# Transposed probabilities of a causal attention: eight tiles a group become six, with V's first 64 tokens copied for the packed half

## The chip, the cores and the metric

The kernel runs on one core of one Trainium2 chip. The metric is the device time of one execution in microseconds (us), as the median of the runs shown.

## The reference, cut to what matters

The program is one transformer layer over 64 sequences ("batches") of 128 tokens and 1024 channels. A token stage builds the input h; then attention and a feed-forward part are added to it:

```
h = tok(log_dt, Lambda, x)                       # 64 x 128 x 1024
h = h + attn(layernorm(h), Wq, Wk, Wv, Wo)
h = h + ffn(layernorm(h), A, B, Wr, br)

# attn: 32 query heads in 8 groups of 4; a group shares one key head and one value head; head size 32
scores = einsum('bhqd,bhkd->bhqk', q, k_h) / sqrt(32)
scores = where(causal, finfo.min, scores)        # query t sees keys 0..t only
attn   = softmax(scores)
ctx    = einsum('bhqk,bhkd->bhqd', attn, v_h)
return ctx @ Wo
```

## The kernel before, in words

A first stage (some 245 us) makes h and the weights. The layer stage then works on one batch of 128 tokens at a time. Values are held as a high and a low f16 part, and products are the sum of three: high by high, high by low and low by high.

The causal mask leaves the first 64 queries with the first 64 keys only. So in each group the scores are computed in four tiles of 128 rows, where a row is one of two heads and one of 64 queries: two *lower* tiles (queries 0 to 63, 64 keys) and two *upper* tiles (queries 64 to 127, 128 keys). One group g of batch b goes through this chain:

1. TensorE: `scores`, four matmuls (L930) of 64, 64, 128 and 128 columns.
2. VectorE: `mask_min`, mask and row minimum, four instructions (L1206).
3. ScalarE: `exps`, four exponentials with their sums (L1062).
4. VectorE: `reciprocals` (L1214).
5. GpSimd: `normalise`, the probabilities by the reciprocals (L1427), over all 512 columns of `pr`. The two stretches of 64 columns that the lower tiles don't fill were set to zero once, before the loop.
6. ScalarE: `p_high`, the f16 part (L1072).
7. GpSimd: `p_low`, the rest in f16 (L1435).
8. The sync queue (SP): `p_transpose`, one DMA transpose of eight 128x128 tiles, four high and four low, into `pt[g]` (L868).

When all eight groups are transposed, `values` (L945) multiplies V by them. The output of a group is 32 rows high, so four groups lie side by side in the array's columns, and a *round* is four matmuls, one for each group. A half of the heads takes three rounds of 512 columns, so a batch takes six rounds, 24 matmuls. `ctx_high` (ScalarE, L1080) and `ctx_low` (VectorE, L1220) take the result, and the output projection (L902 to L904) uses it.

All of it is software-pipelined by hand. Each engine has a `body(i)` that lists the steps of several batches in a fixed order, and semaphores tie the engines. In TensorE's body `values(i - 1)` stands between pieces of the query projection of batch i + 1 (L916). In VectorE's body `reciprocals(i, 4)` is followed by `residual2(i - 3, 0)` (L1338), which empties the bank `pd` after the first three matmuls of the feed-forward output (L1008 to L1010); the second three need that bank.

Of the kernel before, what the change touches and what calls it, by code (L numbers as in the profile page):

```python
# [14 lines left out]
f16 = mybir.dt.float16  # L15
# [4 lines left out]
P = 128  # L20
# [626 lines left out]
def layer_stage(nc, h0, out, W, h_sent, ln_in):  # L647
# [5 lines left out]
    with ExitStack() as ctx:  # L653
# [6 lines left out]
        def ps(name):  # L660
# [25 lines left out]
        vf = sb("vf", [P, G * HD])  # L686
        v_hi = [sb(f"v_hi{i}", [P, G * HD], f16) for i in range(2)]
        v_lo = [sb(f"v_lo{i}", [P, G * HD], f16) for i in range(2)]
        smin = [sb(f"smin{i}", [P, HG]) for i in range(2)]
        pr = [sb(f"pr{i}", [P, HG * P]) for i in range(2)]  # L690
        rsum = [sb(f"rsum{i}", [P, HG]) for i in range(2)]
        rinv = [sb(f"rinv{i}", [P, HG]) for i in range(2)]
        p16 = [sb(f"p16{i}", [P, 2 * HG * P], f16) for i in range(2)]
        pt = [sb(f"pt{i}", [P, 2 * HG, P], f16) for i in range(RP)]
        ctx_t = [sb(f"ctx_t{i}", [P, 2 * G, P], f16) for i in range(2)]
# [61 lines left out]
        kl_done = sem("kl_done")  # L757
        vl_done = sem("vl_done")
        p_norm = sem("p_norm")

        TILES = tuple((h, pair, slice((2 * h + pair) * P, (2 * h + pair) * P + (HT, P)[h]))
                      for h in range(2) for pair in range(HG // 2))

# [30 lines left out]
        with nc.Block() as block:  # L794
# [102 lines left out]
            def _(pe):  # L897
# [36 lines left out]
                def values(b, odd):  # L934
                    if not has(b):
                        return
                    reached(pe, vl_done, 1, b, 1)
                    reached(pe, ctxl_done, G // 4, b)
                    for g in range(G):
                        landed(pe, b, g)  # L940
                    for m in range(G // 4):
                        for n, (v, lo) in enumerate(((v_hi[odd], 0), (v_lo[odd], 0), (v_hi[odd], HG))):
                            for g in range(4 * m, 4 * m + 4):
                                strip = slice(HD * (g % 4), HD * (g % 4) + HD)
                                last = pe.matmul(pv_ps[m][strip, :], v[:, g * HD:(g + 1) * HD],  # L945
                                                 pt[g][:, lo:lo + HG, :], start=(n == 0), stop=(n == 2))
                        last.then_inc(pv_done, 1)
# [105 lines left out]
            def _(act):  # L1053
# [84 lines left out]
                def v_high(b, odd):  # L1138
                    if not has(b):
                        return  # L1140
                    reached(act, kv_used, 1, b, 1)
                    reached(act, pv_done, G // 4, b - 1)
                    A.activation(v_hi[odd][:, :], vf[:, :], ACT.Copy).then_inc(vh_done, 1)

# [51 lines left out]
            def _(dve):  # L1196
# [13 lines left out]
                def reciprocals(b, g):  # L1210
                    if not has(b):
                        return
                    reached(dve, exp_done, G, b, g + 1)
                    V.reciprocal(rinv[g % 2][:, :], rsum[g % 2][:, :]).then_inc(rinv_done, 1)  # L1214
# [153 lines left out]
                def body(i, odd):  # L1368
# [46 lines left out]

                for i in range(2):
                    V.memset(pr[i][:, :].rearrange("p (t k) -> p t k", t=HG)[:, 0:2, HT:P], 0.0)
                bodies(dve, body)

            @block.gpsimd  # L1420
            def _(pool):
                def normalise(b, g):
                    if not has(b):
                        return
                    reached(pool, rinv_done, G, b, g + 1)
                    p3 = pr[g % 2][:, :].rearrange("p (j k) -> p j k", j=HG)
                    nc.gpsimd.tensor_tensor(p3, p3, rinv[g % 2][:, :].unsqueeze(2).broadcast_to([P, HG, P]),  # L1427
                                            ALU.mult).then_inc(p_norm, 1)

                def p_low(b, g):  # L1430
                    if not has(b):
                        return
                    reached(pool, ph_done, G, b, g + 1)
                    p = p16[g % 2]
# [36 lines left out]
                def v_low(b, odd):  # L1471
                    if not has(b):
                        return
                    reached(pool, vh_done, 1, b, 1)
                    nc.gpsimd.tensor_tensor(v_lo[odd][:, :], vf[:, :], v_hi[odd][:, :], ALU.subtract).then_inc(vl_done, 1)

# [61 lines left out]
```

## Time and profile before

| | |
|---|---|
| median of 3 runs | 2345.7 us (2343.22 to 2347.69) |
| the profiled execution's own time | 2347.87 us |
| its span | 2345.8 us |
| batches in the layer stage | 64 |
| granted TensorE clock, mean | 0.984 |

The span is divided by the profile into busy time of the engines. TensorE is busy for 95% of it, VectorE, ScalarE and GpSimd for 74 to 78%. A busy share says how full an engine is, not who waits for whom; for that the waits and the order of time are read. In the rows, PE is TensorE's matmuls, PEld its weight loads, DVE is VectorE, ACT is ScalarE and POOL is GpSimd. A matmul's duration in a row contains the time for which its result is still on the way, so a stream is read by the distance from start to start.

### The profile page before, as it was taken

What the parts mean: (1) busy time and instruction counts of PE and PEld (TensorE: products, weight loads), DVE (VectorE), ACT (ScalarE), POOL (GpSimd) and SP (SyncE); (2) the same over time, 40 slices, a digit from 0 to 9 for tenths busy, and PEclk for the clock granted to TensorE, in tenths of its full rate; (3) what the DMA queues carried; (4) which work ended last, traced back from release to release, by engine and by line L of the source; (5) the groups of instructions that cost most, each with busy time, mean ns of one, the idle gap of its engine ahead of it and who ended that gap; (6) DMA issues with size and microseconds to landing.
All of it is one profiled execution on the core that took longest, in us unless ns stands there. A gap on an engine that the chain in (4) does not pass through costs nothing.

```text
span 2345.8 us, 49764 instructions
## 1 busy us (share of the span) xinstructions
PE 2223.9 (95%) x14040; PEld 1160.3 (49%) x14040; DVE 1831.2 (78%) x7750; ACT 1752.2 (75%) x6141; POOL 1729.0 (74%) x1550
## 2 busy tenths in 40 slices
PE   3998699999999999999999999999999999999985
PEld 2886244544444444544454444444444444444442
DVE  8999467878877787777787778777777778777763
ACT  5887478777777777777877777777777777777772
POOL 3775488777777777777877777777777777777771
PEclk9999799999999999999999999999999999999987
DMA  3988699999999999999999999999999999999993
GB/s 95 291 270 257 118 173 190 188 192 191 186 196 196 187 190 194 193 184 193 197 187 193 194 184 193 193 189 190 191 186 193 200 188 191 194 186 187 184 174 81
DMA packets 1205662, 443.12 MB, mean 189 GB/s; under 512 B 1155718, under 2 KB 1158022, under 8 KB 1205388
## 3 DMA queue, kind: packets, MB, share of 16 engines
q1 hardware_dynamic: 1205380, 439.93, 95.7%
q8 instruction: 114, 1.87, 0.3%
q14 instruction: 160, 1.31, 0.2%
q10 hardware_dynamic: 8, 0.01, 0.0%
HBM read 87.43 MB, written 67.11 MB: 66 GB/s over the span
## 4 chain that ended last, share of the span: by engine, by line
PE 30%; POOL 17%; DMA 15%; DVE 11%; SPq 7%; issue 5%; ACT 4%; POOLq 0%; ACTq 0%; DVEq 0%
DMA pt<-p 11%; POOL p L1435 8%; POOL pr L1427 5%; PE pb L916 5%; PE pa L916 5%; PE pc L916 4%; SPq L868 3%; DMA h_ln<-h 3%; DVE xs L1267 3%; DVE pr L1206 2%; ACT p L1072 2%; POOL qr L1446 2%; PE pb L902 2%; PE pa L902 2%; PE pa L903 2%
## 5 line engine op out<-in xcount | busy, mean ns | idle before, releaser
L1062 ACT ACTIVATE pr<-pr,smin 128x64 f32<-128x64 f32 (+1 forms) x2048 | 737.8, 362 | 181.7 <-DVE smin L1206 180.6
L1427 POOL TENSOR_TENSOR pr<-pr,rinv 128x512 f32<-128x512 f32 x512 | 556.7, 1094 | 369.4 <-DVE rinv L1214 368.8
L1435 POOL TENSOR_TENSOR p<-pr,p 128x512 f16<-128x512 f32 x512 | 590.6, 1158 | 82.4 <-ACT p L1072 81.5
L1206 DVE CUSTOM_DVE_ANT_0 pr<-s_ps,cst 128x64 f32<-128x64 f32 (+1 forms) x2048 | 404.1, 252 | 239.4 <-POOL p L1435 146.2
L1072 ACT ACTIVATE p<-pr 128x512 f16<-128x512 f32 x512 | 320.0, 625 | 267.7 <-DMA pt<-p 146.7
L1062 ACT ACTIVATION_READ_ACCUMULATOR pr<-pr,smin 128x1 f32 x2048 | 383.5, 187 | 0.0
L916 PE MATMUL pa<-wkv_hi,xt 128*128 128x512 f16 x1024 | 326.7, 380 | 17.7 <-DMA xt<-xs 17.7
L916 PE MATMUL pb<-wq_hi,xt 128*128 128x512 f16 x1024 | 327.4, 381 | 0.0
L916 PE MATMUL pc<-wq_hi,xt 128*128 128x512 f16 x1024 | 315.0, 379 | 0.0
L640 PE MATMUL hps<-z,xw 128*128 128x256 f32 x792 | 177.9, 385 | 54.6 <-POOL xw L366 38.2
L902 PE MATMUL pb<-wo_hi,ctx_t 128*128 128x512 f16 x512 | 194.2, 379 | 4.2 <-DVE ctx_t L1220 3.7
L916 PE MATMUL pb<-wq_lo,xt 128*128 128x512 f16 x512 | 195.7, 382 | 0.0
L916 PE MATMUL pa<-wkv_lo,xt 128*128 128x512 f16 x512 | 195.6, 382 | 0.0
L902 PE MATMUL pa<-wo_hi,ctx_t 128*128 128x512 f16 x512 | 194.9, 381 | 0.0
L903 PE MATMUL pa<-wo_lo,ctx_t 128*128 128x512 f16 x512 | 194.8, 380 | 0.0
L904 PE MATMUL pa<-wo_hi,ctx_t 128*128 128x512 f16 x512 | 194.8, 380 | 0.0
L904 PE MATMUL pb<-wo_hi,ctx_t 128*128 128x512 f16 x512 | 194.3, 379 | 0.0
L903 PE MATMUL pb<-wo_lo,ctx_t 128*128 128x512 f16 x512 | 194.3, 379 | 0.0
L916 PE MATMUL pc<-wq_lo,xt 128*128 128x512 f16 x512 | 194.0, 379 | 0.0
L640 PEld LDWEIGHTS hps<-z,xw 128*128 128x128 f32 x792 | 150.9, 192 | 81.2 <-POOL xw L366 44.2
L930 PEld LDWEIGHTS s_ps<-kt,qt 128*128 128x128 f16 x2048 | 121.9, 98 | 130.2 <-DVE smin L1206 30.2
L930 PE MATMUL s_ps<-kt,qt 128*128 128x64 f16 (+1 forms) x2048 | 171.9, 207 | 11.0 <-DVE smin L1206 5.4
(178 smaller groups left out, 4730.2 us busy)
## 6 DMA issues: line engine op xcount, KB each, us to landing
h<-rows SPq DMA_DIRECT2D x128, 256.0 KB, 4.0
h_res<-h SPq DMA_DIRECT2D x64, 512.0 KB, 4.5
out<-rows SPq DMA_DIRECT2D x64, 512.0 KB, 3.3
h_ln<-h SPq DMA_DIRECT2D x63, 512.0 KB, 4.5
pt<-p SPq DMA_TRANSPOSE x512, 4.0
xa<-x SPq DMA_DIRECT2D x16, 256.0 KB, 4.2
xb<-x SPq DMA_DIRECT2D x32, 128.0 KB, 3.9
wst<-wq SPq DMA_DIRECT2D x8, 512.0 KB, 4.8
```

The lines of the kernel that those rows point to most:

```text
L640: last = pe.matmul(hps[t % 4][:, QROW * i:QROW * i + QROW], xw[w % XWR][:, t % WIN, 2 * i:2 * i + 2, :], z[g % ZR][:, 2 * (t % 2) + m, :], ...
L868: sp.dma_start_transpose(pt[g % RP][:, :, :], p16[g % 2][:, :]).then_inc(pt_in[g % RP], 16)
L902: pe.matmul(bank, x[:, k, :], w_hi[:, k, cols], start=(k == 0), stop=False)
L903: pe.matmul(bank, x[:, k, :], w_lo[:, k, cols], start=False, stop=False)
L904: last = pe.matmul(bank, x[:, KC + k, :], w_hi[:, k, cols], start=False, stop=(k == KC - 1))
L916: last = pe.matmul(bank, x[:, k if n < 2 * KC else KC + k, :], w[:, k, cols], start=(n == 0), stop=(n == 3 * KC - 1))
L930: last = pe.matmul(s_ps[g % 2][:, cols], qt[h][:, head:head + 2, :], kt[:, g, 0:HT * h + HT], start=True, stop=True)
L1062: last = A.activation(p, p, ACT.Exp, bias=smin[g % 2][:, j:j + 1], scale=-1.0, accum_out=rsum[g % 2][:, j:j + 1])
L1072: A.activation(p16[g % 2][:, 0:HG * P], pr[g % 2][:, :], ACT.Copy).then_inc(ph_done, 1)
L1206: V.tensor_tensor_reduce(pr[g % 2][:, cols], s_ps[g % 2][:, cols], masks[h], 1.0, 3e38, ALU.add, ALU.min, smin[g % 2][:, j:j + 1]).then_in ...
L1427: nc.gpsimd.tensor_tensor(p3, p3, rinv[g % 2][:, :].unsqueeze(2).broadcast_to([P, HG, P]), ALU.mult).then_inc(p_norm, 1)
L1435: nc.gpsimd.tensor_tensor(p[:, HG * P:], pr[g % 2][:, :], p[:, 0:HG * P], ALU.subtract).then_inc(pl_done, 1)
```

## The change

The transposed input of a group has six tiles in place of eight. The upper tiles keep a high and a low tile each (four). For a lower tile the 64 high columns and the 64 low columns stand side by side in one tile of 128, so two tiles do for the lower half; after the transpose the high part lies on partitions 0 to 63 and the low part on 64 to 127. V's first 64 tokens are therefore put on both halves of the partitions in a new buffer `v_twice`, by two VectorE copies a batch, and one matmul with it sums the high and the low part of the lower tiles. The lower half then needs two rounds (`vt_hi`, `vt_lo`) instead of three. Its second one also adds the product of the two low parts, which was not there before.

So `pr` has no unused columns (384 instead of 512), the order of the four tiles is lower, upper, upper, lower, and `p_high` and `p_low` are two instructions each, one for the upper tiles (256 columns) and one for the lower ones (128).

```diff
-        v_hi = [sb(f"v_hi{i}", [P, G * HD], f16) for i in range(2)]
-        v_lo = [sb(f"v_lo{i}", [P, G * HD], f16) for i in range(2)]
+        v_parts = [sb(f"v_parts{i}", [P, 2, G * HD], f16) for i in range(2)]
+        v_twice = [sb(f"v_twice{i}", [P, 2, G * HD], f16) for i in range(2)]
...
-        pr = [sb(f"pr{i}", [P, HG * P]) for i in range(2)]
+        pr = [sb(f"pr{i}", [P, 6 * HT]) for i in range(2)]
...
-        rinv = [sb(f"rinv{i}", [P, HG]) for i in range(2)]
-        p16 = [sb(f"p16{i}", [P, 2 * HG * P], f16) for i in range(2)]
-        pt = [sb(f"pt{i}", [P, 2 * HG, P], f16) for i in range(RP)]
+        rinv = [sb(f"rinv{i}", [P, HG, 2]) for i in range(2)]
+        p16 = [sb(f"p16{i}", [P, 6 * P], f16) for i in range(2)]
+        pt = [sb(f"pt{i}", [P, 6, P], f16) for i in range(RP)]
...
-        TILES = tuple((h, pair, slice((2 * h + pair) * P, (2 * h + pair) * P + (HT, P)[h]))
-                      for h in range(2) for pair in range(HG // 2))
+        TILES = ((0, 0, slice(0, HT)), (1, 0, slice(HT, 3 * HT)),
+                 (1, 1, slice(3 * HT, 5 * HT)), (0, 1, slice(5 * HT, 6 * HT)))
+
+        def upper(p):
+            return p[:, HT:5 * HT]
+
+        def lower(p):
+            return p[:, :].rearrange("p (n k) -> p n k", k=HT)[:, 0:6:5, :]
+
+        def stacked(p, part):
+            return p[:, 4 * P:6 * P].rearrange("p (n s k) -> p n s k", s=2, k=HT)[:, :, part, :]
...
                 def values(b, odd):
-                    reached(pe, vl_done, 1, b, 1)
+                    reached(pe, vt_done, 1, b, 1)
...
                     for m in range(G // 4):
-                        for n, (v, lo) in enumerate(((v_hi[odd], 0), (v_lo[odd], 0), (v_hi[odd], HG))):
-                            for g in range(4 * m, 4 * m + 4):
-                                strip = slice(HD * (g % 4), HD * (g % 4) + HD)
-                                last = pe.matmul(pv_ps[m][strip, :], v[:, g * HD:(g + 1) * HD],
-                                                 pt[g][:, lo:lo + HG, :], start=(n == 0), stop=(n == 2))
+                        for rounds, cols in ((((v_hi[odd], 0), (v_lo[odd], 0), (v_hi[odd], 2)), slice(2 * P, 4 * P)),
+                                             (((vt_hi[odd], 4), (vt_lo[odd], 4)), slice(0, 2 * P))):
+                            for n, (v, tile) in enumerate(rounds):
+                                for g in range(4 * m, 4 * m + 4):
+                                    strip = slice(HD * (g % 4), HD * (g % 4) + HD)
+                                    last = pe.matmul(pv_ps[m][strip, cols], v[:, g * HD:(g + 1) * HD],
+                                                     pt[g][:, tile:tile + 2, :],
+                                                     start=(n == 0), stop=(n == len(rounds) - 1))
                         last.then_inc(pv_done, 1)
...
-                    A.activation(p16[g % 2][:, 0:HG * P], pr[g % 2][:, :], ACT.Copy).then_inc(ph_done, 1)
+                    A.activation(p16[g % 2][:, 0:2 * P], upper(pr[g % 2]), ACT.Copy).then_inc(ph_done, 1)
+                    A.activation(stacked(p16[g % 2], 0), lower(pr[g % 2]), ACT.Copy).then_inc(ph_done, 1)
...
+                def values_twice(b, odd):
+                    if not has(b):
+                        return
+                    reached(dve, vl_done, 1, b, 1)
+                    V.tensor_copy(v_twice[odd][0:HT, :, :], v_parts[odd][0:HT, :, :])
+                    V.tensor_copy(v_twice[odd][HT:P, :, :], v_parts[odd][0:HT, :, :]).then_inc(vt_done, 1)
...
                     reciprocals(i, 4)
+                    values_twice(i, odd)
                     residual2(i - 3, 0, 1 - odd)
...
-                    nc.gpsimd.tensor_tensor(p3, p3, rinv[g % 2][:, :].unsqueeze(2).broadcast_to([P, HG, P]),
+                    nc.gpsimd.tensor_tensor(p3, p3, by_block.unsqueeze(2).broadcast_to([P, 6, HT]),
                                             ALU.mult).then_inc(p_norm, 1)
...
-                    nc.gpsimd.tensor_tensor(p[:, HG * P:], pr[g % 2][:, :], p[:, 0:HG * P],
-                                            ALU.subtract).then_inc(pl_done, 1)
+                    p, q = p16[g % 2], pr[g % 2]
+                    reached(pool, ph_done, 2 * G, b, 2 * g + 1)
+                    nc.gpsimd.tensor_tensor(p[:, 2 * P:4 * P], upper(q), p[:, 0:2 * P], ALU.subtract)
+                    reached(pool, ph_done, 2 * G, b, 2 * g + 2)
+                    nc.gpsimd.tensor_tensor(stacked(p, 1), lower(q), stacked(p, 0), ALU.subtract).then_inc(pl_done, 1)
```

On TensorE, these rows of the kernel before are `values(i - 1)` in the middle of the query projection (bank `pc`), with one group's scores behind it:

```order
L916 MATMUL pc<-wq_hi,xt 128x512
L916 MATMUL pc<-wq_lo,xt 128x512
L945 MATMUL pv_ps<-pt,v_hi 32x512 x4
L945 MATMUL pv_ps<-pt,v_lo 32x512 x4
L945 MATMUL pv_ps<-pt,v_hi 32x512 x8
L945 MATMUL pv_ps<-pt,v_lo 32x512 x4
L945 MATMUL pv_ps<-pt,v_hi 32x512 x4
L930 MATMUL s_ps<-kt,qt 128x64 x2
L930 MATMUL s_ps<-kt,qt 128x128 x2
```

And the same place in the changed kernel:

```order
L928 MATMUL pc<-wq_hi,xt 128x512
L928 MATMUL pc<-wq_lo,xt 128x512
L959 MATMUL pv_ps<-pt,v_parts 32x256 x12
L959 MATMUL pv_ps<-pt,v_twice 32x256 x8
L959 MATMUL pv_ps<-pt,v_parts 32x256 x12
L959 MATMUL pv_ps<-pt,v_twice 32x256 x8
L942 MATMUL s_ps<-kt,qt 128x64
L942 MATMUL s_ps<-kt,qt 128x128 x2
L942 MATMUL s_ps<-kt,qt 128x64
```

24 matmuls of 512 columns in six rounds of four have become 40 of 256 columns in ten rounds of four. Nothing else moves on TensorE but the order of the four score tiles.

On VectorE, these rows of the kernel before lie between the reciprocals of group 4 and those of group 5, where `residual2` (first and second half) stands:

```order
L1214 RECIPROCAL rinv<-rsum 128x4
L1338 SCALAR_TENSOR_TENSOR rows<-pd,rows 128x512
L1224 BN_STATS bn<-h_ln 128x6 x2
L1228 BN_AGGR mv<-bn 128x2
L1230 TENSOR_SCALAR nrm<-mv 128x1
L1338 SCALAR_TENSOR_TENSOR rows<-pd,rows 128x512
L1214 RECIPROCAL rinv<-rsum 128x4
```

The same place in the changed kernel:

```order
L1230 RECIPROCAL rinv<-rsum 128x8
L1244 COPY v_twice<-v_parts 64x512
L1245 COPY v_twice<-v_parts 64x512
L1362 SCALAR_TENSOR_TENSOR rows<-pd,rows 128x512
L1248 BN_STATS bn<-h_ln 128x6 x2
L1252 BN_AGGR mv<-bn 128x2
L1254 TENSOR_SCALAR nrm<-mv 128x1
L1362 SCALAR_TENSOR_TENSOR rows<-pd,rows 128x512
L1230 RECIPROCAL rinv<-rsum 128x8
```

Two copies stand in the queue ahead of the first `residual2`, and the reciprocals write eight columns instead of four.

## Rows read from the trace of the kernel before

**Rows 1.** Page, part 1: busy time, share of the span, instructions, by engine.
```profile
PE 2223.9 (95%) x14040; PEld 1160.3 (49%) x14040; DVE 1831.2 (78%) x7750; ACT 1752.2 (75%) x6141; POOL 1729.0 (74%) x1550
```

**Rows 2.** Stretch of 400 us: busy of five engines, PEclk, DMA share, GB/s.
```profile
600.00:1000.00 400.00, 398.89 (x2608) 198.28 (x2606) 315.21 (x1477) 309.40 (x1122) 312.65 (x291) 1.00 1.02 192
```

**Rows 3.** TensorE in order of time, start and duration in us, at L945 of one batch.
```profile
1224.20 0.40 PE L945 MATMUL pv_ps<-pt,v_hi 128*32 128x512 f16 x4
1224.42 0.39 PE L945 MATMUL pv_ps<-pt,v_lo 128*32 128x512 f16 x4
...
1225.29 0.39 PE L945 MATMUL pv_ps<-pt,v_hi 128*32 128x512 f16 x4
1225.61 0.34 PE L930 MATMUL s_ps<-kt,qt 128*128 128x64 f16 x4
1225.79 0.38 PE L916 MATMUL pc<-wq_hi,xt 128*128 128x512 f16 x1
```

**Rows 4.** TensorE's weight loads in order of time, same place.
```profile
1224.21 0.10 PEld L945 LDWEIGHTS pv_ps<-pt,v_lo 128*32 128x32 f16 x4
```

**Rows 5.** TensorE in order of time: matmuls of 136 columns, six steps apart.
```profile
1210.24 0.22 PE L902 MATMUL pd<-aw_hi,x2t 128*128 128x136 f16 x1
...
1210.59 0.22 PE L902 MATMUL pd<-aw_hi,x2t 128*128 128x136 f16 x1
```

**Rows 6.** Chain that ended last, in order of time: start, us, matmuls of 512 columns.
```profile
1225.95 3.88 PE pc L916 x18
```

**Rows 7.** TensorE in order of time: first round of `values` of two other batches.
```profile
1255.80 0.40 PE L945 MATMUL pv_ps<-pt,v_hi 128*32 128x512 f16 x4
...
2179.80 0.40 PE L945 MATMUL pv_ps<-pt,v_hi 128*32 128x512 f16 x4 [0.34 <-DMA pt<-p]
```

**Rows 8.** L945 from 360 to 2200 us: duration min/median/max, first and last start.
```profile
L945 PE MATMUL pv_ps<-pt,v_hi x928: 376/379/392, 366.2 to 2180.9; 128*32 128x512 f16 x186
```

**Rows 9.** TensorE's waits, 600 to 2200 us: us in total, times, longest.
```profile
PE pv_ps L945 <- DMA pt<-p: 5.8, 8, 1.3
...
PE pd L1008 <- DVE rows L1338: 0.5, 1, 0.5
```

**Rows 10.** Waits from 2230 us to the end.
```profile
PE pv_ps L945 <- DMA pt<-p: 8.2, 2, 4.6
```

**Rows 11.** Page, part 5: busy, mean ns of one, idle before, and who ended it.
```profile
L1427 POOL TENSOR_TENSOR pr<-pr,rinv 128x512 f32<-128x512 f32 x512 | 556.7, 1094 | 369.4 <-DVE rinv L1214 368.8
L1435 POOL TENSOR_TENSOR p<-pr,p 128x512 f16<-128x512 f32 x512 | 590.6, 1158 | 82.4 <-ACT p L1072 81.5
...
L1072 ACT ACTIVATE p<-pr 128x512 f16<-128x512 f32 x512 | 320.0, 625 | 267.7 <-DMA pt<-p 146.7
```

**Rows 12.** Groups by line and shape, same columns: 256 and 128 columns.
```profile
L1475 POOL TENSOR_TENSOR v_lo<-vf,v_hi 128x256 f16<-128x256 f32 x64 | 42.9, 671 | 0.0
...
L1143 ACT ACTIVATE v_hi<-vf 128x256 f16<-128x256 f32 x64 | 25.6, 400 | 0.0
...
L1157 ACT ACTIVATE ls_hi<-pd 128x128 f16<-128x128 f32 x64 | 16.5, 257 | 1.4 <-PE pd L1000 1.4
```

**Rows 13.** Page, part 6: DMA issues, count, median us from issue to landing.
```profile
pt<-p SPq DMA_TRANSPOSE x512, 4.0
...
kt<-ks SPq DMA_TRANSPOSE x128, 2.5
```

**Rows 14.** L1314 from 600 to 2200 us: duration ns min/median/max.
```profile
L1314 DVE COPY ks<-ks x50: 287/498/537, 609.7 to 2169.3; 128x512 f16<-128x512 f16 x50
```

**Rows 15.** VectorE in order of time at the first `residual2` of one batch.
```profile
1234.20 0.18 DVE L1214 RECIPROCAL rinv<-rsum 128x4 f32<-128x4 f32 x1
1234.74 0.69 DVE L1338 SCALAR_TENSOR_TENSOR rows<-pd,rows 128x512 f32<-128x512 f32 x1 [0.36 <-PE pd L1010]
```

**Rows 16.** TensorE in order of time: second three matmuls into `pd`.
```profile
1236.49 0.38 PE L1008 MATMUL pd<-bm_hi,ls_hi 128*128 128x512 f16 x1
```

**Rows 17.** Chain that ended last: the transpose before a late `values`.
```profile
1696.66 6.20 DMA pt<-p
```

More of the change, by code:

```diff
@@ L686, in layer_stage @@
         vf = sb("vf", [P, G * HD])
-        v_hi = [sb(f"v_hi{i}", [P, G * HD], f16) for i in range(2)]
-        v_lo = [sb(f"v_lo{i}", [P, G * HD], f16) for i in range(2)]
+        v_parts = [sb(f"v_parts{i}", [P, 2, G * HD], f16) for i in range(2)]
+        v_twice = [sb(f"v_twice{i}", [P, 2, G * HD], f16) for i in range(2)]
+        v_hi, v_lo = ([a[:, n, :] for a in v_parts] for n in range(2))
+        vt_hi, vt_lo = ([a[:, n, :] for a in v_twice] for n in range(2))
         smin = [sb(f"smin{i}", [P, HG]) for i in range(2)]
-        pr = [sb(f"pr{i}", [P, HG * P]) for i in range(2)]
+        pr = [sb(f"pr{i}", [P, 6 * HT]) for i in range(2)]
         rsum = [sb(f"rsum{i}", [P, HG]) for i in range(2)]
-        rinv = [sb(f"rinv{i}", [P, HG]) for i in range(2)]
-        p16 = [sb(f"p16{i}", [P, 2 * HG * P], f16) for i in range(2)]
-        pt = [sb(f"pt{i}", [P, 2 * HG, P], f16) for i in range(RP)]
+        rinv = [sb(f"rinv{i}", [P, HG, 2]) for i in range(2)]
+        p16 = [sb(f"p16{i}", [P, 6 * P], f16) for i in range(2)]
+        pt = [sb(f"pt{i}", [P, 6, P], f16) for i in range(RP)]
         ctx_t = [sb(f"ctx_t{i}", [P, 2 * G, P], f16) for i in range(2)]
@@ L758, in layer_stage @@
         vl_done = sem("vl_done")
+        vt_done = sem("vt_done")
         p_norm = sem("p_norm")
-        TILES = tuple((h, pair, slice((2 * h + pair) * P, (2 * h + pair) * P + (HT, P)[h]))
-                      for h in range(2) for pair in range(HG // 2))
+        TILES = ((0, 0, slice(0, HT)), (1, 0, slice(HT, 3 * HT)),
[6 more added lines that the diff above has]
+            return p[:, 4 * P:6 * P].rearrange("p (n s k) -> p n s k", s=2, k=HT)[:, :, part, :]
         def in_halves(bank):
@@ L1142, in v_high @@
                     reached(act, pv_done, G // 4, b - 1)
-                    A.activation(v_hi[odd][:, :], vf[:, :], ACT.Copy).then_inc(vh_done, 1)
+                    A.activation(v_hi[odd], vf[:, :], ACT.Copy).then_inc(vh_done, 1)
                 def router_exp(b):
@@ L1213, in reciprocals @@
                     reached(dve, exp_done, G, b, g + 1)
-                    V.reciprocal(rinv[g % 2][:, :], rsum[g % 2][:, :]).then_inc(rinv_done, 1)
+                    V.reciprocal(rinv[g % 2][:, :, :],
+                                 rsum[g % 2][:, :].unsqueeze(2).broadcast_to([P, HG, 2])).then_inc(rinv_done, 1)
                 def ctx_low(b, m, odd):
@@ L1413, in body @@
                         x_low(0, i + 3, 0)
-                for i in range(2):
-                    V.memset(pr[i][:, :].rearrange("p (t k) -> p t k", t=HG)[:, 0:2, HT:P], 0.0)
                 bodies(dve, body)
@@ L1425, in normalise @@
                     reached(pool, rinv_done, G, b, g + 1)
-                    p3 = pr[g % 2][:, :].rearrange("p (j k) -> p j k", j=HG)
-                    nc.gpsimd.tensor_tensor(p3, p3, rinv[g % 2][:, :].unsqueeze(2).broadcast_to([P, HG, P]),
+                    p3 = pr[g % 2][:, :].rearrange("p (n k) -> p n k", k=HT)
+                    by_block = rinv[g % 2][:, :, :].rearrange("p j s -> p (j s)")[:, 1:7]
+                    nc.gpsimd.tensor_tensor(p3, p3, by_block.unsqueeze(2).broadcast_to([P, 6, HT]),
                                             ALU.mult).then_inc(p_norm, 1)
@@ L1432, in p_low @@
                         return
-                    reached(pool, ph_done, G, b, g + 1)
-                    p = p16[g % 2]
-                    nc.gpsimd.tensor_tensor(p[:, HG * P:], pr[g % 2][:, :], p[:, 0:HG * P],
-                                            ALU.subtract).then_inc(pl_done, 1)
+                    p, q = p16[g % 2], pr[g % 2]
[3 more added lines that the diff above has]
+                    nc.gpsimd.tensor_tensor(stacked(p, 1), lower(q), stacked(p, 0), ALU.subtract).then_inc(pl_done, 1)
                 def sum_q(b, half):
@@ L1474, in v_low @@
                     reached(pool, vh_done, 1, b, 1)
-                    nc.gpsimd.tensor_tensor(v_lo[odd][:, :], vf[:, :], v_hi[odd][:, :], ALU.subtract).then_inc(vl_done, 1)
+                    nc.gpsimd.tensor_tensor(v_lo[odd], vf[:, :], v_hi[odd], ALU.subtract).then_inc(vl_done, 1)
                 def body(i, odd):
```

## The prediction, on record before the changed kernel ran

> **What bounds the kernel now.** I read the busy shares first: TensorE 95%, the other three 74 to 78% [rows 1]. A share alone doesn't say who waits, so I took a stretch in the middle, free of start and end: TensorE is busy for 398.89 of 400 us at the full clock of 2.4 GHz, VectorE, ScalarE and GpSimd for 309 to 315, and the DMA share is 1.02 [rows 2]. The reader is to see two candidates, TensorE and the DMA rings. The order of time decides between them. From one batch's first round of `values` to the next batch's is 31.60 us (1224.20 to 1255.80) [rows 3, 7]. Over 57 such steps (928 matmuls with `v_hi` are 58 batches of 16; 366.2 to 2179.80) the mean is 31.82 [rows 7, 8]. So a batch costs TensorE 31.60 us of back-to-back work, and all waiting adds 0.22 us, some 14 us over 64 batches. The DMA rings are full but keep up. Two things count then: columns taken from TensorE's stream, which are worth their time 64 times, and what shortens the waits, which can be worth 14 us at most in the steady part.
>
> **TensorE's rounds.** The four matmuls of a round start together and the next round starts 0.22 us later (1224.20, 1224.42) [rows 3], the pitch of a single full-width matmul of 512 columns, 3.88 / 18 = 0.2156 us [rows 6]. So a round costs what one matmul costs. For 136 columns the pitch is (1210.59 - 1210.24) / 6 = 0.058 us [rows 5]. Pitch by columns is then a line, (0.2156 - 0.058) / 376 = 0.00042 us a column, and 256 columns come to 0.1085 us. Before: 6 x 0.2156 = 1.293 us. After: 10 x 0.1085 = 1.085 us. That is -0.208 us a batch, -13.3 us for 64. The 0.1 us at either end, where narrow and full-width tiles meet (the stretch is 1.41 us, from 1224.20 to 1225.61), stays.
>
> What this needs is that 40 pairs of a weight load and a matmul pass at 0.027 us a pair. The trace has no stretch of that density that long. The bound from above: four score matmuls pass in 0.18 us (1225.61 to 1225.79), 0.045 each [rows 3], so 40 would take 1.80 us, +0.51 a batch, +32 us. The bound from below is the line. I take the line, for two reasons: by the line the score matmuls' 384 columns alone come to 0.166 of their 0.18 us, so they are paced by columns and not by their number; and the four loads of the second round begin at 1224.21, 0.01 us after the first round's four matmuls, so eight loads and four matmuls had been handed over by then [rows 3, 4], while a round of 0.1085 us needs only eight instructions.
> The Trainium skill speaks against the change here: "TensorE: Matmul & The Clock Gate", section on 56 ns against 53.3 ns, says that with hardware decode off the sequencer spends some 62 ns on each matmul, which binds when the array's work is shorter. By that rule 40 matmuls would be an estimated 2.48 us, and the change 76 us slower. The trace disagrees already: matmuls of 136 columns pass at 58 ns and the scores at 45.
>
> **The group's chain.** GpSimd's price goes by columns: 1158 ns for 512, 671 for 256 [rows 11, 12], 0.0019 us a column. `normalise` loses 128 columns, -0.24 us. `p_high` and `p_low` were 0.625 + 1.158 = 1.78 us in a row [rows 11]. Now the first part of `p_high` (0.400 for 256 columns), the first of `p_low` (0.671) and the second of `p_low` (0.671 - 0.243 = 0.428) are in a row, 1.50 us; the second `p_high` (0.257 for 128 columns, read from PSUM, the nearest row) lies beside the first `p_low` [rows 12]. That is -0.28 us. The transpose of eight tiles lands after 4.0 us, the one of four after 2.5 [rows 13], 0.375 us a tile, so six tiles give -0.75; the bound is nothing, if the rings' backlog sets the landing. Sum: a group's chain is 1.27 us shorter, at least 0.52. Per batch GpSimd gives back 8 x 0.30 = 2.4 us; ScalarE gains 8 x 0.03 = 0.3 us, which its 23% of idle time covers.
>
> Where that is worth something: `values` needs all eight groups, and TensorE waits for the last transposes 5.8 us in 1600 us, 8 times, at most 1.3 us each [rows 9]. One such place shows a landing that took 6.20 us from the end of `p_low` [rows 17], so the backlog matters and is relieved by two tiles in eight. Waits of at most 1.3 us against a chain shorter by 1.27: I let 6 of the 7 us go that this makes over all batches (5.8 x 2000 / 1600 = 7.3). At the end of the program TensorE waits 8.2 us in two places [rows 10]; each gets one chain's shortening, -2.5 us in all. The start, where the first groups run without other work, is left at nothing.
>
> **VectorE's copies.** Two copies of 64 x 512 f16 stand ahead of the first `residual2`. The nearest row, a copy of 128 x 512 f16 in SBUF, takes 287 to 537 ns [rows 14], so the two take 0.57 to 1.07 us. The reciprocal of eight columns instead of four adds nothing that counts. The cover: VectorE is idle for 0.36 us before `residual2` because it waits for `pd`; `residual2` then ends at 1234.74 + 0.69 = 1235.43, and the matmuls that need the bank start at 1236.49, 1.06 us later [rows 15, 16]. Cover 1.42 us against 0.57 to 1.07: nothing on the path in this batch. In others VectorE comes later: TensorE waited once for this step, 0.5 us [rows 9]. Behind the copies in VectorE's queue are `residual2`, the statistics of the next input, and the reciprocals of group 5, for which GpSimd waits; the shorter chain gives that group more than the copies take. I charge 0.03 us a batch, +2 us; the ends are nothing, and 0.3 us a batch (+19) if the dear price comes with a late VectorE. `values` waits for the copies instead of `v_lo`; they are done almost a batch ahead.
>
> **Sum.** -13.3 - 6 - 2.5 + 2 = -19.8 us against the profiled execution's 2347.9, so 2328.1. That execution lies 2.2 us above the median of the runs, 2345.7, so the median becomes 2326.
>
> **The rivals.**
> *More than that.* All waits of the steady part go (-14 instead of -6) and the start gains too, some 3 us: 2315. For it: the rings are the fullest resource, and a quarter of the largest group of transposes leaves them. Against: some waits belong to ctx and `pd`, which the change doesn't shorten. 0.14.
> *The copies eat it.* At 1.07 us a batch and with VectorE late, `residual2` holds back the second half of the feed-forward output by some 0.3 us a batch: 2343, no change. For it: the one wait there, and copies that vary by a factor of two. Against: 1.42 us of cover, and no work after it that depends on the exact place. 0.10.
> *Slower: narrow rounds are paced by their number.* If a pair costs as much as a score matmul, 0.045 us, `values` takes 1.80 us: +32 - 8.5 + 2 = +26, so 2371. It decides from 1.293 / 40 = 0.0323 us a pair on (no gain from the rounds), and the kernel is slower as a whole from about 0.035. For it: no stretch of the trace shows 80 instructions at this rate. Against: the density at the start of a round [rows 3, 4]. 0.08. At 0.062 us a pair the same mechanism would give 2.48 us, 2415; rows at 0.045 and 0.058 leave that 0.01 of the 0.08. That price is the one of the Trainium skill's page "TensorE: Matmul & The Clock Gate" cited above.
> *The rounds gain and the waits only move.* ScalarE's extra instruction or VectorE's later reciprocals cost what the chain gained: only -13.3, and some of that given back: 2333 to 2340, still faster. 0.18, taken into the forecast's lower side.
> The forecast itself, 2320 to 2333: 0.50.
>
> **How the numbers follow.** A measurement of this kernel tells about 0.2% (4.7 us) from no change, so faster means below 2341. Forecast, "more" and "only move" are all faster, 0.82; the copies give 0.10 around no change; the paced rounds and what I don't see give 0.08 slower. The range for 8 in 10 reaches from "more", 2314, to where the copies begin to eat the gain, 2342.
>
> **What would show it.** The starts of the rounds of `values`: 0.109 us apart, first round to the scores 1.20 us instead of 1.41. A batch to batch distance of 31.39 us where undisturbed, and a mean of 31.5 to 31.6. TensorE's wait for `pt` at `values` under 2 us in the same 1600. The landing of `pt` near 3.3 us, `normalise` near 0.86 us. `residual2` no later than 1.4 us after its reciprocals, and no new wait of TensorE for `rows`. It would be wrong if the rounds are over 0.13 us apart, or if waits for `rows` by the matmuls into `pd` add up to over 10 us.

## The result, and the profile after

The changed kernel took 2316.7 us in the median (2315.72 to 2318.0) against 2346.7 us for the kernel before in the same comparison, ratio 0.9866, 95% interval 0.9851 to 0.9882: 30 us faster. The forecast was 2326 and 20 us faster. Its direction and its range held, the latter near its fast end; it was a third too small, and the runs below show that the reason is not only a size.

The page of the changed kernel: span, part 1 and the first DMA queue (its share is that of the time of the core's 16 DMA engines in the span; the text calls these engines the rings), and the landing of the transposes:

```profile
span 2315.4 us, 52962 instructions
...
PE 2204.1 (95%) x15064; PEld 1187.6 (51%) x15064; DVE 1882.6 (81%) x7876; ACT 1744.2 (75%) x6653; POOL 1548.6 (67%) x2062
...
q1 hardware_dynamic: 1074308, 406.38, 89.1%
...
pt<-p SPq DMA_TRANSPOSE x512, 3.6
```

The mean granted clock is 0.985, against 0.984 before. Against [rows 1] TensorE's share is the same and GpSimd's has fallen by 180 us. The transposes land after 3.6 us instead of 4.0 [rows 13]. The rings' share was 95.7% of 2345.8 us before and is 89.1% of 2315.4: 182 us less for 1024 tiles less (two in each of 512 groups), 0.18 us of all rings a tile (by the other pairs of runs below that differ in tiles it is 0.17 to 0.20).

TensorE in order of time at `values`, to be laid beside [rows 3], and the first rounds of the next batch and of one late in the program:

```profile
1180.43 0.51 PE L959 MATMUL pv_ps<-pt,v_parts 128*32 128x256 f16 x12
1180.77 0.39 PE L959 MATMUL pv_ps<-pt,v_twice 128*32 128x256 f16 x8
1180.99 0.50 PE L959 MATMUL pv_ps<-pt,v_parts 128*32 128x256 f16 x12
1181.31 0.39 PE L959 MATMUL pv_ps<-pt,v_twice 128*32 128x256 f16 x8
1181.64 0.34 PE L942 MATMUL s_ps<-kt,qt 128*128 128x64 f16 x4
...
1211.83 0.40 PE L959 MATMUL pv_ps<-pt,v_parts 128*32 128x256 f16 x8
...
2185.34 0.51 PE L959 MATMUL pv_ps<-pt,v_parts 128*32 128x256 f16 x12
```

Five rounds of 256 columns lie between 1180.43 and 1180.99, two between 1180.77 and 1180.99: 0.11 us each. The stretch to the scores is 1.21 us instead of 1.41. An undisturbed batch is 31.40 us (1180.43 to 1211.83) instead of 31.60. And the mean is close to it now. `values` from 360 to 2200 us:

```profile
L959 PE MATMUL pv_ps<-pt,v_parts x1416: 272/273/284, 362.5 to 2186.1; 128*32 128x256 f16 x177
```

1416 / 24 = 59 batches, 58 steps from 362.5 to 2185.34: 31.43 us, against 31.82 [rows 7, 8]. So of 0.39 us a batch, 25 us over 64, 0.20 is the rounds and 0.19 is waiting that has gone. TensorE's waits from 600 to 2200 us, for [rows 9], are one row, and the stretch for [rows 2] has the rings' share at 0.95 instead of 1.02:

```profile
PE pd L1023 <- DVE rows L1362: 0.6, 1, 0.6
```
```profile
600.00:1000.00 400.00, 399.28 (x2854) 205.31 (x2853) 327.81 (x1518) 312.50 (x1240) 278.92 (x396) 1.00 0.95 176
```

The other 5 us are the start (the first `values` began at 305.7 us before and begins at 303.2) and the end. The start's part isn't shown to be the change's: in the profiled executions of all the runs below that moment lies between 303.8 and 307.4 us, and six tiles in the kernel before put it at 307.4. The question for the experiments is which part of the change took the waits away, and whether the rounds' 13 us are the rounds' own.

### The profile page after: what moved, and what is told of

Read it like the earlier page. It is cut to its first block, busy times and chain, and to the rows that moved or that the text cites. A ratio compares the mean times of both kernels' runs of the same rounds, so it can differ in the third digit from the quotient of the medians.

```text
span 2315.4 us, 52962 instructions
## 1 busy us (share of the span) xinstructions
PE 2204.1 (95%) x15064; PEld 1187.6 (51%) x15064; DVE 1882.6 (81%) x7876; ACT 1744.2 (75%) x6653; POOL 1548.6 (67%) x2062
## 3 DMA queue, kind: packets, MB, share of 16 engines
q1 hardware_dynamic: 1074308, 406.38, 89.1%
## 4 chain that ended last, share of the span: by engine, by line
PE 83%; DVE 2%; DMA 2%; ACT 1%; issue 1%; SPq 1%; POOL 1%; POOLq 0%; DVEq 0%; ACTq 0%
PE pb L928 14%; PE pa L928 14%; PE pc L928 13%; PE pb L914 5%; PE pb L916 5%; PE pb L915 5%; PE pa L915 5%; PE pa L914 5%; PE pa L916 5%; PE s_ps L942 4%; PE pv_ps L959 3%; PE pd L1023 1%; PE pd L914 1%; PE pd L916 1%; PE pd L1025 1%; PE pd L915 1%
## 5 line engine op out<-in xcount | busy, mean ns | idle before, releaser
L1077 ACT ACTIVATE pr<-pr,smin 128x128 f32<-128x128 f32 (+1 forms) x2048 | 738.3, 362 | 234.5 <-DVE smin L1222 233.9
L1451 POOL TENSOR_TENSOR pr<-pr,rinv 128x384 f32<-128x384 f32 x512 | 449.4, 879 | 550.9 <-DVE rinv L1230 544.4
L1222 DVE CUSTOM_DVE_ANT_0 pr<-s_ps,cst 128x128 f32<-128x128 f32 (+1 forms) x2048 | 403.6, 252 | 200.0 <-PE s_ps L942 101.7
L1459 POOL TENSOR_TENSOR p<-pr,p 128x256 f16<-128x256 f32 x512 | 343.6, 671 | 34.1 <-ACT p L1087 30.2
L1087 ACT ACTIVATE p<-pr 128x256 f16<-128x256 f32 x512 | 209.7, 410 | 175.7 <-POOL pr L1451 110.1
L1461 POOL TENSOR_TENSOR p<-pr,p 128x128 f16<-128x128 f32 x512 | 219.0, 428 | 0.0
L942 PEld LDWEIGHTS s_ps<-kt,qt 128*128 128x128 f16 x2048 | 136.0, 98 | 113.9 <-DVE smin L1222 18.3
```

Source lines behind the costliest of these rows:

```text
L942: last = pe.matmul(s_ps[g % 2][:, cols], qt[h][:, head:head + 2, :], kt[:, g, 0:HT * h + HT], start=True, stop=True)
L1077: last = A.activation(p, p, ACT.Exp, bias=smin[g % 2][:, j:j + 1], scale=-1.0, accum_out=rsum[g % 2][:, j:j + 1])
L1087: A.activation(p16[g % 2][:, 0:2 * P], upper(pr[g % 2]), ACT.Copy).then_inc(ph_done, 1)
L1222: V.tensor_tensor_reduce(pr[g % 2][:, cols], s_ps[g % 2][:, cols], masks[h], 1.0, 3e38, ALU.add, ALU.min, smin[g % 2][:, j:j + 1]).then_in ...
L1451: nc.gpsimd.tensor_tensor(p3, p3, by_block.unsqueeze(2).broadcast_to([P, 6, HT]), ALU.mult).then_inc(p_norm, 1)
L1459: nc.gpsimd.tensor_tensor(p[:, 2 * P:4 * P], upper(q), p[:, 0:2 * P], ALU.subtract)
```

## The experiments

Each was timed in at least 3 rounds beside the kernel before. The mean step from batch to batch is over 59 steps of the profiled execution, from the second batch on, worked out from the starts of `values` as above. It is 31.82 us in the kernel before and 31.41 in the changed one (31.43 above, over 58 steps from the third batch on). A profiled execution can lie a few us beside its kernel's median, and 6 us are 0.1 us a step. Tiles are those of one group's transpose. The kernel before had medians of 2345.4, 2349.5 and 2348.2 us beside three sets of these runs, so small differences are read from the ratios.

| run | what | median us | ratio to before (95%) | mean step us |
|---|---|---|---|---|
| b_split | before, 12 rounds of 256 | 2350.6 | 1.0021 (1.0010 to 1.0031) | 31.90 |
| b_five | before, 5 of 6 rounds | 2347.9 | 1.0006 (0.9995 to 1.0016) | 31.75 |
| b_tiles6 | before, 6 tiles | 2333.0 | 0.9929 (0.9904 to 0.9954) | 31.59 |
| b_six_five | before, both | 2321.1 | 0.9885 (0.9867 to 0.9904) | 31.39 |
| b_tiles9 | before, 9 tiles | 2391.9 | 1.0195 (1.0169 to 1.0221) | 32.50 |
| a_tiles8 | changed, 8 tiles | 2353.4 | 1.0028 (1.0014 to 1.0042) | 31.97 |
| a_chain | changed, longer GpSimd chain | 2378.7 | 1.0137 (1.0122 to 1.0152) | 32.34 |
| a_both | changed, 8 tiles and longer chain | 2394.6 | 1.0193 (1.0172 to 1.0214) | 32.58 |
| a_nocopy | changed, no copies | 2318.5 | 0.9868 (0.9848 to 0.9888) | 31.38 |
| a_copy3x | changed, six copies | 2400.4 | 1.0221 (1.0198 to 1.0244) | 32.72 |
| a_tiles8_nocopy | changed, 8 tiles, no copies | 2346.5 | 0.9997 (0.9986 to 1.0008) | 31.88 |
| a_chain_nocopy | changed, longer chain, no copies | 2321.1 | 0.9883 (0.9865 to 0.9901) | 31.41 |

### Are narrow rounds paced by columns? (b_split)

```diff
-  for n, (v, lo) in enumerate(((v_hi[odd], 0), (v_lo[odd], 0), (v_hi[odd], HG))):   # 512 columns
+  for half in (1, 0):
+      cols = slice(2 * P * half, 2 * P * half + 2 * P)                              # 256 columns
+      for n, (v, lo) in enumerate(((v_hi[odd], 0), (v_lo[odd], 0), (v_hi[odd], HG))):
```

> The kernel before, with the six rounds of 512 columns of the values' product cut into twelve of 256: the same columns, 48 matmuls instead of 24. If narrow rounds are paced by columns, as the line through the pitches says, twelve of 0.1085 us are 1.302 us against 1.293: +0.6 us over 64 batches, so no change. If a pair of a weight load and a matmul has a price of its own, of 0.032 us or more, it is at least +0.24 us a batch, +15 us.

It was 0.21% slower, 5 us, with the undisturbed step at 31.61 us instead of 31.60. The undisturbed step answers the question: 48 matmuls in place of 24 cost 0.01 us a batch. The rest is in batches that are disturbed (a mean of 31.90, 0.29 us above the undisturbed step, against 0.22 before), and no run says why. The theory of a price for each pair falls.

### TensorE's columns alone (b_five)

```diff
-  for n, (v, lo) in enumerate(((v_hi[odd], 0), (v_lo[odd], 0), (v_hi[odd], HG))):
+  three = ((v_hi[odd], 0), (v_lo[odd], 0), (v_hi[odd], HG))
+  for n, (v, lo) in enumerate(three[:3 - m]):
```

> The kernel before, with one of the six rounds of 512 columns left out (the high V by low P product of one half of the heads is not added). That takes 0.2156 us a batch from TensorE, close to the 0.204 that the change takes, and leaves GpSimd, ScalarE, VectorE and the DMA as before. If TensorE's columns alone give the gain, it is the whole -30 us. If the columns give 13.8 us and the waits stay what they are, 13 us in the steady part, -14 us. If a faster TensorE runs into the transposes, waits grow and it is less, -5 to -12.

No change in the median: 1.0006. TensorE's undisturbed step fell to 31.38 us, but the mean step only from 31.82 to 31.75, and even that is mostly the luck of the execution: the profiled one took 2342.9 us, 5.0 below the kernel's median, which is 0.08 us a batch. At the median the step is an estimated 31.83 us (31.75 + 5.0 / 64), as before. In the same 1600 us TensorE now waits 6.4 us for `pt` and 5.3 for `ctx_t`, where it was 5.8 [rows 9] and 1.1. The kernel before, then b_five:

```profile
PE pb L902 <- DVE ctx_t L1220: 1.1, 6, 0.2
```
```profile
PE pv_ps L946 <- DMA pt<-p: 6.4, 8, 1.8
PE pb L902 <- DVE ctx_t L1221: 5.3, 15, 0.4
PE pd L1009 <- DVE rows L1339: 1.4, 3, 0.5
```

This is the run that the prediction did not foresee. A cut in TensorE's columns that is slightly larger than the change's is worth nothing in the kernel before: it is at a second limit, near 31.8 us.

### The tiles of the transpose (b_tiles6, a_tiles8, b_tiles9)

```diff
-  sp.dma_start_transpose(pt[g % RP][:, :, :], p16[g % 2][:, :])
+  sp.dma_start_transpose(pt[g % RP][:, 0:6, :], p16[g % 2][:, 0:6 * P])     # b_tiles6
```
```diff
-  p16 = [sb(f"p16{i}", [P, 6 * P], f16) for i in range(2)]
-  pt = [sb(f"pt{i}", [P, 6, P], f16) for i in range(RP)]
+  p16 = [sb(f"p16{i}", [P, 8 * P], f16) for i in range(2)]                  # a_tiles8; 9 in b_tiles9, on the kernel before
+  pt = [sb(f"pt{i}", [P, 8, P], f16) for i in range(RP)]
```

> The kernel before, with a DMA transpose of six of the eight tiles of a group; the last two tiles of the buffer are set to zero once, so the low part of two of the four probability tiles is left out of the output. TensorE's columns, GpSimd and ScalarE stay. If the DMA tiles are what the waits hung on, the waits of the steady part (13 us) nearly go and start and end gain some 3 us: -12 to -16 us. If the engines' chain is, -0 to -3 us.

> The changed kernel, but each group's DMA transpose has eight tiles again; the two added ones carry zeros that nobody reads. If the waits went because the DMA rings carry a quarter less of these transposes, the steady part's waits come back, +8 to +12 us, and the start and the end lose 2 to 4 us. If they went because of the shorter work of GpSimd and ScalarE, it is +0 to +3 us in all. Batch to batch, undisturbed, stays at 31.395 us either way.

> The kernel before with nine tiles a transpose, the ninth all zeros and read by nobody. Two tiles fewer took 6.6 points from the share of the rings (95.7% to 89.1% of the span), 0.18 us of all rings a tile, so one more tile in eight groups is 1.4 us of ring time a batch. If the rings are the limit at eight tiles, the batch gets longer by nearly that: 33.0 to 33.3 us, +75 to +95 us. If the rings only add latency to the last transposes, a landing later by 0.2 to 0.4 us: +5 to +20 us.

Six tiles in the kernel before: 16.5 us faster, and TensorE waits for nothing at all between 600 and 2200 us; the mean step is its undisturbed one. It was just over what the tiles' theory gave. Its stretch and its queue's row:

```profile
600.00:1000.00 400.00, 400.00 (x2625) 199.24 (x2627) 324.31 (x1482) 311.73 (x1124) 313.84 (x293) 1.00 0.94 176
...
q1 hardware_dynamic: 1074308, 406.38, 87.7%
```

Eight tiles in the changed kernel: 37 us slower than the changed kernel, over twice what I had written (+10 to +16), and slower than the kernel before, although GpSimd and TensorE have less to do. TensorE waits in three places:

```profile
PE pd L1023 <- DVE rows L1362: 12.8, 21, 1.6
PE pv_ps L959 <- DMA pt<-p: 6.0, 10, 1.3
PE pb L914 <- DVE ctx_t L1237: 2.0, 9, 0.3
```

Nine tiles: the step grows by 0.68 us, 44 us in all, between what a hard limit (1.4 us) and mere latency (a fifth of that) would give. So the tiles are a soft limit. The step goes 31.59, 31.82, 32.50 us for six, eight and nine tiles: +0.11 a tile, then +0.68, while the landing's median hardly moves (3.4, 4.0 and 4.1 us). At six tiles the step is TensorE's own, so 0.11 is what is left of the price of a tile above that floor. The median landing is a poor gauge of how full the transposes' path is. The share of the rings says it better (0.94, 1.02 and 1.05 in the same stretch).

What these runs vary is the number of tiles, and it fills two things at once. One is the rings. The other is the sync queue (SP), which issues all transposes one behind the other. The transposes of `pt` on it, from 600 to 2200 us, with the duration of one issue (ns, min/median/max), for six, eight and nine tiles in the kernel before:

```profile
L869 SPq DMA_TRANSPOSE pt<-p x404: 1209/1237/2685, 606.2 to 2194.8; - x135
```
```profile
L868 SPq DMA_TRANSPOSE pt<-p x402: 1231/1528/3475, 599.3 to 2198.9; - x134
```
```profile
L868 SPq DMA_TRANSPOSE pt<-p x394: 1277/1776/3906, 604.2 to 2199.3; - x197
```

The shortest issue hardly grows with the tiles, the median by half a microsecond, which for the eight of a batch makes some 3 to 4 us. Added up over all instructions of the queue, SP is taken for 85, 92 and 95% of that time (87% in the changed kernel). So the full resource may be the rings, which then hold the issues up, or the queue that issues. No run changes one without the other. Where this text says that the rings are full, it means this path of the transposes.

### Both cuts together (b_six_five)

The edits of b_tiles6 and b_five in one kernel.

> The kernel before with both cuts that were tried apart: six of eight tiles transposed (the last two are zeros) and one of six rounds of 512 columns left out. Apart they gave -16.5 us and nothing. If the two are limits side by side, the DMA rings at some 31.8 us a batch and TensorE's columns at 31.60, then with the rings relieved the columns count: batch to batch 31.38 us, -28 to -31 us, as the changed kernel. If each is worth what it was alone, -15 to -19 us. If the shorter engine steps of the changed kernel are needed too, batch to batch stays above 31.5.

Apart they gave 16.5 us and nothing, together 27 us (ratio 0.9885), with the step at 31.39 us. The rounds count only once the rings are relieved. This kernel has none of GpSimd's shorter steps, so those are not needed for the 27 us. Its step is the changed kernel's; the 3 us that the change gains beyond it lie in the start and the end, and no run divides them (the two intervals overlap). Read the other way round, from b_six_five to b_five, two tiles cost 27 us when TensorE has the shorter stream, against 16.5 with the longer one. This kernel leaves out part of the output, and only shows where the time is.

```profile
600.00:1000.00 400.00, 400.00 (x2597) 199.04 (x2596) 326.76 (x1495) 314.63 (x1135) 315.52 (x294) 1.00 0.94 176
```

### The engines' chain and the copies (a_chain, a_both, a_nocopy, a_copy3x)

```diff
-  pr = [sb(f"pr{i}", [P, 6 * HT]) for i in range(2)]
+  pr = [sb(f"pr{i}", [P, 8 * HT]) for i in range(2)]                        # a_chain: normalise over 512
...
   nc.gpsimd.tensor_tensor(p[:, 2 * P:4 * P], upper(q), p[:, 0:2 * P], ALU.subtract)
+  nc.gpsimd.tensor_tensor(pad[g % 2][:, :], q[:, HT:2 * HT], p[:, 0:HT], ALU.subtract)
```
```diff
-  values_twice(i, odd)                                                      # a_nocopy, vt_hi and vt_lo lie in v_parts
...
+  four more of V.tensor_copy(v_more[n][0:HT, :, :], v_parts[odd][0:HT, :, :])   # a_copy3x
```

> The changed kernel, with the group's chain on GpSimd as long as before: normalise over 512 columns again (+0.21 us) and a dummy subtraction of 64 columns between the two of p_low (+0.3 us). The DMA keeps six tiles. If the shorter work of the engines took the waits away, they come back, +8 to +12 us. If the DMA tiles did it, +0 to +3 us. If each did half and either is enough, both this run and the one with eight tiles show little.

> The changed kernel with eight tiles a transpose and with GpSimd's longer chain together. Left of the change are TensorE's fewer columns and the copies. All theories of the waits expect them back: +14 to +18 us against the changed kernel, so about -13 us against the one before, the columns' share. If it stays faster than that by over 5 us, something else that the change did takes waits away (the finer steps of p_high and p_low).

> The changed kernel without the two copies on VectorE: the lower half's product takes V's tokens where they lie, so the low parts of those probabilities meet the wrong tokens. If the copies cost nothing on the path, as the trace's cover of 1.4 us says, 0 to -1 us. If they held TensorE as the prediction charged, -2 us.

> The changed kernel with four more copies of the same size ahead of the two, into buffers that nobody reads: six instead of two. At 0.3 to 0.5 us each that is 1.2 to 2 us more on VectorE a batch. If the cover of 1.42 us is what hides the copies, it is used up: TensorE waits for residual2 at the matmuls into pd, 0.3 to 1 us a batch, +20 to +60 us. If VectorE's slack is elsewhere too and TensorE is simply far from it, +0 to +5 us.

Of the four expectations only that of a_nocopy was met; a_copy3x went the way of its first theory, but further than its 20 to 60 us. The longer chain cost 62 us, five times the most that I had allowed, and with eight tiles 78 us, less than the sum of both alone (62 and 37). Taking the copies out of the changed kernel changes nothing (2318.5 against 2316.7 us, ratios 0.9868 and 0.9866). Tripling them costs 84 us. The waits name the same place in both kernels; first a_chain, then a_copy3x:

```profile
PE pd L1024 <- DVE rows L1363: 37.9, 50, 1.1
PE pb L915 <- DVE ctx_t L1238: 0.8, 2, 0.5
```
```profile
PE pd L1024 <- DVE rows L1367: 57.1, 49, 1.8
```

The place is `residual2` behind the copies, in each of some 50 batches. VectorE in order of time in the changed kernel, GpSimd's `normalise` beside it, and TensorE's matmul that needs the bank:

```profile
1189.59 0.20 DVE L1230 RECIPROCAL rinv<-rsum 128x8 f32<-128x8 f32 x1
1189.71 0.28 DVE L1244 COPY v_twice<-v_parts 64x512 f16<-64x512 f16 x1
1190.00 0.84 DVE L1245 COPY v_twice<-v_parts 64x512 f16<-64x512 f16 x1
1190.88 0.69 DVE L1362 SCALAR_TENSOR_TENSOR rows<-pd,rows 128x512 f32<-128x512 f32 x1
```
```profile
1189.87 0.83 POOL L1451 TENSOR_TENSOR pr<-pr,rinv 128x384 f32<-128x384 f32 x1
```
```profile
1192.52 0.38 PE L1023 MATMUL pd<-bm_hi,ls_hi 128*128 128x512 f16 x1
```

In the changed kernel the two copies are the same operation on the same source. The first takes 0.28 us, the second 0.84, because `normalise`, which the reciprocals ahead of them release, starts on GpSimd at 1189.87, before the second copy, and the second copy doesn't end before it: `normalise` ends at 1190.70, the copy at 1190.84. One thing differs between the two: the second writes the other half of the partitions. The six copies of a_copy3x rule that out as the cause. VectorE in one batch, then GpSimd:

```profile
1227.50 0.93 DVE L1246 COPY v_more<-v_parts 64x512 f16<-64x512 f16 x1
1228.36 1.24 DVE L1247 COPY v_more<-v_parts 64x512 f16<-64x512 f16 x1
...
1229.72 0.28 DVE L1249 COPY v_twice<-v_parts 64x512 f16<-64x512 f16 x1
1230.01 0.29 DVE L1250 COPY v_twice<-v_parts 64x512 f16<-64x512 f16 x1
```
```profile
1227.46 0.83 POOL L1456 TENSOR_TENSOR pr<-pr,rinv 128x384 f32<-128x384 f32 x1
1228.25 1.20 POOL L1483 TENSOR_TENSOR qs<-qr,qs 128x512 f16<-128x512 f32 x1
```

The dear ones write the first half, each ends 0.14 or 0.15 us behind an instruction of GpSimd, and the copy to the other half (L1250) takes 0.29 us with GpSimd idle.

The changed kernel's two copies take 1.12 us together, and `residual2` ends at 1191.57, 0.95 us before TensorE needs `pd`. In a_chain `normalise` has 512 columns and the copy lasts longer too:

```profile
1217.70 0.23 DVE L1223 CUSTOM_DVE_ANT_0 pr<-s_ps,cst 128x64 f32<-128x64 f32 x1 [1.76 <-POOL p L1466]
...
1219.69 0.20 DVE L1231 RECIPROCAL rinv<-rsum 128x8 f32<-128x8 f32 x1
1219.81 0.40 DVE L1245 COPY v_twice<-v_parts 64x512 f16<-64x512 f16 x1
1220.22 1.04 DVE L1246 COPY v_twice<-v_parts 64x512 f16<-64x512 f16 x1
1221.29 0.69 DVE L1363 SCALAR_TENSOR_TENSOR rows<-pd,rows 128x512 f32<-128x512 f32 x1
```
```profile
1222.13 0.38 PE L1024 MATMUL pd<-bm_hi,ls_hi 128*128 128x512 f16 x1 [0.65 <-DVE rows L1363]
```

Here VectorE has already waited 1.76 us for the longer `p_low`, against 1.17 at the same place in the changed kernel, and comes to the copies late; the reader sees a chain from GpSimd through VectorE's queue to TensorE. The run overshoots in one respect. From the start of `normalise` to the end of `p_low` its group takes about what it took before (2.91 against 2.88 us by the means of the steps), but GpSimd itself works 2.50 us a group, against 2.25 before and 1.98 in the changed kernel. So its 62 us can't be taken as the price of the lost length of the chain alone.

### The copies taken out again (a_tiles8_nocopy, a_chain_nocopy)

Each is the run above with the edit of a_nocopy.

> The changed kernel with eight tiles a transpose and without VectorE's copies (the low parts of the lower tiles meet the wrong tokens). With eight tiles and the copies a batch took 31.97 us in the mean, with eight tiles and five rounds in the kernel before 31.75. If the copies are the difference, this run comes to 31.75 and 2337 to 2343 us. If the copies cost nothing here either, it stays at 31.95, 2350 to 2355 us.

> The changed kernel with GpSimd's longer chain and without the copies. With the copies it was 62 us slower than the changed kernel, and TensorE waited for residual2 in every batch. If that cost goes through the copies, which stand ahead of residual2 and last longer beside GpSimd's work, nearly all of it goes: 2315 to 2325 us. If the longer chain itself holds VectorE up, it stays over 2350.

Without the copies the longer chain costs 2.6 us (2321.1 against 2318.5, with overlapping intervals) instead of 62. That settles where its price was: in what stands behind the copies. With eight tiles the copies are worth 7 us of the 37: TensorE's wait at `pd` goes from 12.8 us to 1.0. The rest, 28 us (2346.5 against 2318.5; 30 by the ratios), are the rings' own, as the 27 between b_six_five and b_five at the same columns of TensorE. The mean step of 31.88 is above b_five's 31.75, but the medians are 2346.5 and 2347.9 us: that gap is the fast execution in which b_five was profiled. With the copies out, then, the changed kernel with eight tiles is as slow as the kernel before, though GpSimd and TensorE have less to do: the shorter steps and the fewer rounds gain nothing while the tiles stay.

## Why the prediction was right, and where it was not

**The rounds: right in size, incomplete in condition.** 0.1085 us a round was predicted, 0.11 is in the trace, and the undisturbed step fell by 0.20 us as worked out. b_split confirms the line at 256 columns. The rival of paced pairs is refuted, and a price of 62 ns a matmul doesn't show here: 40 pairs pass in about 1.1 us, 27 ns each. But the step "columns taken from TensorE's stream ... are worth their time 64 times" failed: b_five takes the columns alone and gains nothing. "The DMA rings are full but keep up" was the wrong reading of [rows 2]: the share of 1.02 went with a second limit near 31.8 us, at the mean step of the kernel before and 0.2 above TensorE's own. That the rounds' 13 us came all the same is owed to the tiles, which the same change took away and which the working of this term doesn't mention; so far it was luck.

**The waits: right in part, half the size.** The term was 6 of some 14 us; 12 went (0.19 us a batch). They were put down to a group's chain shorter by 1.27 us, with the transposes as one part. The runs separate them: six tiles alone remove all of the waits, and the longer engine chain without the copies brings back none (31.41 us). So of the 1.27 us the 0.75 of the landing named the right thing, and the 0.52 of the engines' steps bought nothing. The working took only TensorE's waits that carry the transposes' name, 5.8 us; with six tiles those for `ctx_t` and `rows` go as well, so they hang on the transposes too, by a way that no row here traces. The rival "more than that", 2315 us, came nearest, and its reason, the transposes that leave the rings, is what the runs show. What it held against itself, that the waits for ctx and `pd` would stay, was wrong.

**The chain of the group.** `normalise` was predicted at 0.86 us and takes 0.88 in the mean, the two `p_low` 0.67 and 0.43 as worked out. The two `p_high` take 0.41 and 0.29 where 0.400 and 0.257 were taken, so ScalarE has 0.08 us a group more to do and not 0.03. The landing was predicted at 3.3 and is 3.6. What was wrong is what the engines' part of this is worth: nothing by itself, but it keeps room for the copies.

**The copies: the bounds were too low, the outcome was right by luck of cover.** 0.57 to 1.07 us were the ends; they take 1.13 (0.28 + 0.84), since the second is held until GpSimd's `normalise` is over. The cost on the path is nothing, not 2 us. "No work after it that depends on the exact place" was wrong: the margin is 0.95 us in the batch shown, and a_chain's longer GpSimd work uses it up in every batch. The sentence "the shorter chain gives that group more than the copies take" pointed at what matters: with a_chain's longer work the changed kernel loses 32 us to the kernel before, and without the copies it loses next to nothing of its gain. How much a chain of just the old length would cost isn't measured, since a_chain overshoots it.

**Start and end.** The end was charged -2.5; start and end together gave 5, of which the start's 2.5 lie within what single executions differ by.

The sum was 10 us short: 6 by the waits, 2 by the copies, 2 to 3 by start and end.

## What to carry to other kernels

Where two resources are near full, the gains of relieving each don't add: here one cut alone moved nothing, the other 16.5 us, and both together 27. Before crediting a shorter stream, look for a second row at its limit in the same stretch, here the DMA share beside TensorE's busy time, and take its step, not zero, as the floor. An instruction put ahead of a wait is safe by the margin behind it at that place, and that margin belongs to the speed of the other engines; note what else would use it up. And price a VectorE copy by what GpSimd does at the same time, not by its size alone.

## What the runs showed of the hardware that was not expected

- A 64 x 512 f16 copy on VectorE takes 0.28 us with GpSimd idle (a_copy3x) and 0.84 us when GpSimd's `normalise` of 128 x 384 f32 starts ahead of it, 1.04 us beside one of 128 x 512. All 64 second copies of the changed kernel lie between 0.82 and 0.89 us; the second row is a_chain's:

```profile
L1245 DVE COPY v_twice<-v_parts x64: 823/841/892, 285.3 to 2256.1; 64x512 f16<-64x512 f16 x64
```
```profile
L1246 DVE COPY v_twice<-v_parts x64: 1037/1040/1108, 286.7 to 2317.1; 64x512 f16<-64x512 f16 x64
```

- Transposes near their limit slow this program gradually: from a share of the rings of 1.02 on, one more tile of 128x128 f16 (0.18 us of all rings) in each of eight groups cost 0.68 us a batch; from 0.94 to 1.02 it was some 0.11 a tile, and 0.2 where TensorE's stream was shorter (27 us for two tiles over 64 batches). Whether rings or issuing queue set this is open.
- Rounds of four matmuls of 32 output rows and 256 columns pass every 0.11 us with their weight loads, eight instructions a round, for ten rounds in a row.
- Entering and leaving the 32-row rounds costs TensorE 0.09 and 0.11 us (0.31 us from 1180.12 to 1180.43 for a matmul of 512 columns that needs 0.22, and 0.33 us from 1181.31 to 1181.64 for two rounds that need 0.22):

```profile
1180.12 0.38 PE L928 MATMUL pc<-wq_lo,xt 128*128 128x512 f16 x1
```

  The Trainium skill, "TensorEngine Tiling (Array Packing)", section "Key Properties", says that a change of the tiling mode drains the engine. The trace agrees in that both changes cost time, 0.09 and 0.11 us; the drain itself is not in its rows.
